# A two-layer graph network on one core: splitting the edge features beforehand and rearranging the attention layer

## The chip, the cores and the metric

The kernel runs on one core of one Trainium2 chip. The core's engines work side by side, each through its own queue of instructions: TensorE (PE), VectorE (DVE), ScalarE (ACT), GpSimd (POOL) and SyncE (SP, which here only issues DMAs). They wait for one another through semaphores. A time is the device time of one execution in microseconds.

## What is computed

A graph of N = 6250 nodes with 16 features, E = 206250 directed edges (each node has a loop edge), 230 edge types. The edges come sorted by dst. Cut to what matters, with h a layer norm and relu of x ahead of each layer:

```python
# layer 0
h_tan = log_map_zero(h)
msg = exp_map_zero(einsum('ei,eio->eo', h_tan[src], rel_weight[etype]) + rel_emb[etype])
lam = 2.0 / (1.0 - c * sum(msg * msg) + EPS)
numer = segment_sum(w * lam * msg, dst);  denom = segment_sum(w * lam, dst)
x = x + mobius_add(project(numer / denom), exp_map_zero(h_tan @ loop_weight))
# layer 1
w_m = (efeat @ W_msg + b_msg).reshape(E, 16, 16);  w_a = (efeat @ W_attn + b_attn).reshape(E, 16, 16)
e1 = w_m * h[src][:, :, None];  e2 = w_a * h[src][:, :, None]
ex = exp(e2 - segment_max(e2, dst)[dst])
attn = ex / segment_sum(ex, dst)[dst]
x = x + segment_sum(e1 * attn, dst).sum(axis=1)
```

## The kernel before

**Tiling.** The nodes are ordered by falling degree into groups of 128, one node to a partition. A window is one group and up to S = 48 consecutive edges of each of its nodes (edge slots, along the free axis). There are 50 windows, run as 25 pairs: the loop body is written out for q = 0 and q = 1, and q chooses the buffer. How many slots a window uses is read from a table (48 in the first, 23 in the last). A block is BLK = 6 slots, a half HALF = 3.

**Prologue** (to about 541 us). TensorE makes a table with one row of 16 floats for each pair of source node and edge type, and SP writes it to DRAM. Index lists srcp (source of each edge) and pairp (row of each edge in that table) are written too, and the raw edge features are copied in DRAM, with 48 rows of padding, into efp (12.9 MB).

**Layer 0** (about 541 to 2935 us). In window k GpSimd waits for the list of indices blkidx, issues 18 gathers (L325, one for each slot, 64 bytes to each partition), then waits for bst_ready and loads blkidx of the window after with pair_block (L320), and issues the rest of the gathers. VectorE, in order: reads the window's word of the table, writes valid (L893), waits for the block load of window k, computes the start and the remainder for window k + 1 (window_start, L873 to L880, which ends in the signal bst_ready), waits for the gathers of window k, and does the math (L903 to L926; ScalarE gives a square root and a tanh in its midst). The signal l0_math at L921 lets GpSimd gather into that buffer again, two windows on. window_start reads two values from the table into registers of VectorE's queue.

**Layer 1** (about 3110 us to the end). Features, weights and biases are split into three bf16 parts each (hi, mid, lo), so that one bf16 product of KE = 100 rows gives fp32 accuracy: hi stands three times, mid twice, lo once, and four more columns carry three ones and the sign of an unused slot (urow makes its score very low). Work of window k:
- GpSimd: the subtraction residue (L376), the loads of source numbers and raw features of the window after (edge_block, L362 and L364), the gathers of rows of h (L325, one for each slot), between them last_part (L380, the low part of the split), at the end the scatter of the finished rows of two windows before (L392).
- ScalarE: the copies of the split (L611, L614), six copies of transposed features from PSUM (L620), the exponential of the carried factor (L633), one exponential for each block of scores (L637, L641).
- TensorE: for each half the attention weights into PSUM (L490), beside them the sums of the exponentials of the window before (exp_sums, L496, products with an identity that add up in the bank psS); then all 48 transposes of the window after (L484), then for each block the message weights and the sums of products (prod_sums, L501).
- VectorE: edge_ids of the window after (L995 to L1000), mold (the maximum carried from the window before, or a very low number where a group begins, L1038), three copies for the finish (L1039 to L1041), window_start two windows ahead, then a score block at a time: two products of weights by h (L1049) and the running maximum (L1061, L1065, L1068). After that the maximum over six slots (L1070), mnew and diff (L1072, L1073), and finish for the window before (L1007 to L1019: total, the sums carried from window to window, is scaled and the sums of psS are added; then ratio and the row of the output). Then the message blocks: scores less maximum (L1089), two products with the message weights (L1049), and their product with the exponentials (L1099), which TensorE adds up.

The order of all engines is written out by hand.

## Time and profile before

| | |
|---|---|
| median of three runs | 6593.14 us (6592.74, 6593.14, 6606.66) |
| the profiled run | 6588.29 us, span 6586.6 us |
| PE busy | 2729.8 us (41%), 13477 instructions |
| PE weight load busy | 1922.8 us (29%) |
| DVE busy | 3678.9 us (56%), 4670 |
| ACT busy | 1293.7 us (20%), 1247 |
| POOL busy | 4382.1 us (67%), 3814 |
| TensorE clock granted | 0.92 on average |
| DMA | 167.76 MB; in layers 0 and 1 some 6 to 12 GB/s |

The span is from the first to the last instruction of the profiled execution; the run took 1.7 us more. Busy is time in which an engine works on an instruction that is not a register, branch, semaphore or DMA-queue one, so time that a queue spends on those is idle time with the reason "issue". The stages have their own limits, so the shares over the whole span say little: they are to be read by stretch.

### The profile page before, as it was taken

How to read it: one execution, taken by the hardware profiler on the slowest of the kernel's cores; microseconds unless marked ns; L12 is line 12 of the kernel's file. 1: busy time of each engine (PE TensorE's matmuls, PEld its weight loads, DVE VectorE, ACT ScalarE, POOL GpSimd, SP SyncE). 2: the span in 40 equal slices, each digit the busy share in tenths (PEclk: the TensorE clock that was granted, in tenths of full speed). 3: DMA queues.
4: the chain of work that ended last, by engine and by line, in shares of the span. 5: the costliest groups of instructions: out<-in, count | busy, mean ns of one | idle time of the engine just before them, and what ended most of it. 6: DMA issues, size and time to landing. Idle time of an engine off the chain costs nothing.

```text
span 6586.6 us, 56916 instructions
## 1 busy us (share of the span) xinstructions
PE 2729.8 (41%) x13477; PEld 1922.8 (29%) x13478; DVE 3678.9 (56%) x4670; ACT 1293.7 (20%) x1247; POOL 4382.1 (67%) x3814
## 2 busy tenths in 40 slices
PE   3530000000000000000567777777777777777676
PEld 1110000000000000000445555555555555555454
DVE  8221111111112111231689989998988898888877
ACT  3530000000000000000222222222222222223222
POOL 0335676767666766656477877777777777776753
PEclk9999999999999999998788888888888888888888
DMA  5880000000000000000000000000000000000000
GB/s 164 275 263 11 6 6 6 6 6 6 6 6 6 6 6 6 6 8 11 6 10 10 12 9 9 9 9 12 9 9 12 9 12 9 12 12 9 12 11 5
DMA packets 141814, 167.76 MB, mean 25 GB/s; under 512 B 73235, under 2 KB 130056, under 8 KB 135287
## 3 DMA queue, kind: packets, MB, share of 16 engines
q0 software_dynamic: 122896, 57.46, 6.2%
q1 hardware_dynamic: 18865, 110.05, 5.2%
q8 instruction: 8, 0.13, 0.0%
q14 instruction: 13, 0.11, 0.0%
q10 hardware_dynamic: 32, 0.01, 0.0%
HBM read 71.76 MB, written 108.57 MB: 27 GB/s over the span
## 4 chain that ended last, share of the span: by engine, by line
POOL 23%; issue 18%; DVE 17%; DVEq 16%; PE 13%; DMA 4%; another core or an unknown queue 4%; POOLq 2%; ACT 1%; SPq 0%; ACTq 0%
POOL gath L325 20%; DVEq L1096 6%; PE psS L501 4%; PE psS L496 4%; DVE stage L1049 4%; PE psW L490 3%; DMA table<-arena 3%; DVEq L1057 3%; DVE arena L1049 2%; DVE work L1070 2%; DVEq L1049 1%; DVE stage L1099 1%; DVE work L673 1%; DVE work L1013 1%
## 5 line engine op out<-in xcount | busy, mean ns | idle before, releaser
L325 POOL DMA_INDIRECT gath<-h_dram,hidx x1695 | 2223.5, 1312 | 509.3 <-issue 509.1
L325 POOL DMA_INDIRECT gath<-table,blkidx x1646 | 1600.0, 972 | 505.7 <-issue 503.0
L484 PE MATMUL psT<-identb,stage 128*100 128x128 bf16 x2448 | 209.5, 255 | 2599.5 <-POOL stage L380 2569.7
L501 PE MATMUL psS<-stage,ident 128*128 128x256 f32 x3390 | 976.3, 447 | 341.8 <-DVE stage L1099 297.7
L484 PEld LDWEIGHTS psT<-identb,stage 128*100 128x100 bf16 x2448 | 190.8, 155 | 2623.9 <-POOL stage L380 2531.5
L501 PEld LDWEIGHTS psS<-stage,ident 128*128 128x128 f32 x3390 | 736.5, 225 | 534.3 <-DVE stage L1099 354.0
L496 PE MATMUL psS<-arena,ident 128*128 128x256 f32 x3390 | 830.4, 382 | 0.0
L490 PE MATMUL psW<-wst,stage 100*128 100x256 bf16 x3390 | 580.0, 292 | 472.2 <-DVE stage L1049 270.0
L673 DVE TENSOR_TENSOR work<-gath 128x768 f32<-128x768 f32 x50 | 47.9, 958 | 1154.1 <-DMA gath<-table,blkidx 1150.8
L496 PEld LDWEIGHTS psS<-arena,ident 128*128 128x128 f32 x3390 | 605.5, 191 | 70.2
L1049 DVE TENSOR_TENSOR arena<-psW,gath 128x768 f32 (+1 forms) x565 | 520.7, 952 | 173.8 <-DMA gath<-h_dram,hidx 58.2
L637 ACT ACTIVATE arena<-arena x271 | 401.9, 1483 | 1019.3 <-DVE arena L1089 989.4
L1099 DVE TENSOR_TENSOR stage<-stage,arena x294 | 498.6, 1696 | 88.7 <-issue 35.3
L620 ACT COPY stage<-psT 100x1024 bf16<-100x1024 bf16 x306 | 289.9, 1026 | 1298.8 <-PE psT L484 1213.6
L1049 DVE TENSOR_TENSOR stage<-psW,gath 128x768 f32 x565 | 513.9, 949 | 24.8 <-remote 24.8
L1089 DVE TENSOR_TENSOR arena<-arena,work 128x1536 f32 (+1 forms) x294 | 496.8, 1690 | 16.2 <-issue 16.2
L490 PEld LDWEIGHTS psW<-wst,stage 100*128 100x128 bf16 x3390 | 287.2, 101 | 725.5 <-DVE stage L1049 325.8
L595 ACT ACTIVATE work<-work 128x48 f32<-128x48 f32 x50 | 12.1, 243 | 2236.7 <-DVE work L905 2092.1
L1065 DVE TENSOR_TENSOR work<-work,arena 128x1536 f32<-128x1536 f32 x171 | 328.6, 1922 | 15.8
L874 DVE SCALAR_TENSOR_TENSOR bstf<-tabs,info 128x1 f32 (+1 forms) x103 | 21.7, 211 | 472.0 <-issue 472.0
L446 PE MATMUL psW<-stage,work 102*125 102x460 bf16 (+1 forms) x400 | 190.9, 617 | 173.1 <-ACT arena L578 141.4
L376 POOL TENSOR_TENSOR efraw<-efraw,stage 128x768 f32<-128x768 f32 x51 | 86.3, 1692 | 236.2 <-DVEq L1000 173.7
(216 smaller groups left out, 2680.3 us busy)
## 6 DMA issues: line engine op xcount, KB each, us to landing
table<-arena SPq DMA_DIRECT2D x50, 1610.0 KB
gath<-h_dram,hidx POOLq DMA_INDIRECT x1695
gath<-table,blkidx POOLq DMA_INDIRECT x1646
efp<-in_edge_attr SPq DMA_DIRECT2D x1, 12890.6 KB
table<-arena SPq DMA_DIRECT2D x50, 186.9 KB
arena<-first_dram POOLq DMA_DIRECT2D x1, 915.5 KB, 12.1
info<-info_dram POOLq DMA_DIRECT2D x2, 432.0 KB, 6.4
arena<-in_dst,rowi POOLq DMA_INDIRECT x51
```

Of the source, the lines that this page charges most:

```text
L325: pool.indirect_dma_start(out=gath[:, q, s, :], out_offset=None, in_=rows, in_offset=bass.IndirectOffsetOnAxis(ap=idx[:, q, s:s + 1].bitca ...
L484: last = nc.tensor.transpose(psTb[0:KE, t % 3, j, 0:GP], efs[:, 8 * t + j, :], identb[0:GP, 0:GP])
L490: last = nc.tensor.matmul(psW[0:GP, h % 2, j * IO:(j + 1) * IO], efT[:, q, h * HALF + j, 0:GP], wst[:, c0:c0 + IO], start=True, stop=True)
L496: nc.tensor.matmul(psS[0:GP, 0:IO], ident[0:GP, 0:GP], score[:, q, s, :], start=False, stop=False)
L501: nc.tensor.matmul(psS[0:GP, IO:2 * IO], ident[0:GP, 0:GP], prod[:, c0:c0 + IO], start=False, stop=False)
L620: nc.scalar.copy(efT[:, q, 8 * t:8 * t + 8, 0:GP], psTb[0:KE, t % 3, :, 0:GP]).then_inc(m["efT_sb"], 1)
L637: nc.scalar.activation(v, v, ACT.Exp).then_inc(m["exp_done"], 1)
L1049: V.tensor_tensor(dst_ap.rearrange("p s (i o) -> p s i o", o=D), psW[0:GP, s, 0:HALF * IO].rearrange("p (s i o) -> p s i o", i=D, o=D), bc ...
L1065: V.tensor_tensor(macc, macc, score[:, q, ds(b * BLK, BLK), :], ALU.max)
L1089: V.tensor_tensor(blk, blk, mnew[:, q, :].unsqueeze(1).to_broadcast([GP, n, IO]), ALU.subtract).then_inc(m["sub_done"], 1)
L1096: V.drain()
L1099: V.tensor_tensor(pr, pr, blk.rearrange("p s c -> p (s c)"), ALU.mult).then_inc(m["q_ready"], 1)
```

## The change

The split of the edge features into bf16 parts no longer happens in each window of layer 1. A new DRAM array ef6 holds, for each edge, its 100 bf16 values (41 MB in all). It is made in 50 chunks during the loop of layer 0: SP loads a chunk of raw features (33 edges to each of 125 partitions), VectorE splits it in four operations behind the math of each window (split_chunk), SP stores it. srcp holds the source number plus one, row 0 of h's array in DRAM is zeros, and unused slots point there. In layer 0 window_start is computed one window earlier.

In layer 1 GpSimd has no arithmetic any more: it loads the source numbers (src_block) and the finished 100-column rows (edge_rows, 9600 bytes to each partition), gathers and scatters. Starts and remainders come from ScalarE (edge_start), and so does mold. The 48 transposes are cut into six parts; two go ahead of the message blocks and one behind the weights of each of the first four blocks, with two PSUM buffers in place of three. ScalarE does the copy of a part behind the exponential of a block. The maximum mnew lies in PSUM. The carried sums are put back into the bank psS by one product of the identity with carry, so the addition to total is gone; the finish follows the first subtraction of the message blocks, and the table's word for the next window is read under its reciprocal. The reduction over six slots has become pairwise maxima, and the three copies at the window's start are gone. The diff, cut to its core and with twelve columns of indentation taken off:

```diff
+        mold, ratio, diff, cfac = (col256(j) for j in range(4))
...
+        carry = efraw[:, 0, 0:2 * IO]
...
+        mnew = psT[0:GP, 8:10, :].rearrange("p a n -> p (a n)")
...
-sp.dma_start(efp_d[0:E * D].rearrange("(a b) -> a b", b=1375),
-             efeat.rearrange("e d -> (e d)").rearrange("(a b) -> a b", b=1375)).then_inc(m["efp_out"], 16)
...
+def chunk_in(rows, j):
+    sp.dma_start(efc[:, j, :, :].rearrange("p r d -> p (r d)"), rows).then_inc(m[f"efc_in{j}"], 16)
+def chunk_out(rows, j):
+    sp.dma_start(rows, ef6[:, j, :, :].rearrange("p r k -> p (r k)")).then_inc(m[f"ef6_out{j}"], 16)
+for j in range(2):
+    chunk_in(efrows[:, j, :], j)
+with sp.Fori(0, ECH // 2 - 1) as t:
+    for j in range(2):
+        sp.wait_ge(m["ef6_split"], t * 2 + (j + 1))
+        chunk_out(ef6rows[:, ds(2 * t + j, 1), :].rearrange("p a n -> p (a n)"), j)
+        chunk_in(efrows[:, ds(2 * t + (j + 2), 1), :].rearrange("p a n -> p (a n)"), j)
...
+def src_block(q):
     pool.indirect_dma_start(out=blkidx[:, q, :], out_offset=None, in_=srcp_d.rearrange("(e a) -> e a", a=1),
...
+                            in_offset=bass.IndirectOffsetOnAxis(ap=ebst[:, q:q + 1].bitcast(U32), axis=0)).then_inc(m[f"src_in{q}"], 16)
+def edge_rows(q):
+    pool.indirect_dma_start(out=efrow, out_offset=None, in_=ef6_d.rearrange("(e k) -> e k", k=KE),
+                            in_offset=bass.IndirectOffsetOnAxis(ap=ebst[:, q:q + 1].bitcast(U32), axis=0)).then_inc(m["ef_in"], 16)
...
-    nc.gpsimd.tensor_tensor(efres, efin, efs[:, :, HI:HI + D], ALU.subtract).then_inc(m["res_done"], 1)
...
-    nc.gpsimd.tensor_tensor(efs[:, :, LO:LO + D], efres, efs[:, :, MID:MID + D], ALU.subtract).then_inc(m["lo_done"], 1)
...
+def next_ids(w, q):
+    pool.wait_ge(m["start_ready"], w + 1)
+    pool.sem_inc(m["passed"], 1)
+    src_block(q)
...
-        residue(k)
-        edge_block(k + 1, 1 - q)
...
-                last_part(k)
+            if b == 1:
+                if q:
+                    next_ids(k + 1, 0)
+                else:
+                    with pool.If(i > 0):
+                        next_ids(k + 1, 1)
...
+        pool.wait_ge(m["efT_ps"], k * (S // 8) + (S // 8))
+        pool.sem_inc(m["passed"], 1)
+        edge_rows(1 - q)
...
+def transposes(w, t):
+    pe.wait_ge(m["efT_sb"], w * (S // 8) + (t + 1))
+    for j in range(8):
+        last = nc.tensor.transpose(psTb[0:KE, t % 2, j, 0:GP], efs[:, 8 * t + j, :], identb[0:GP, 0:GP])
+    last.then_inc(m["efT_ps"], 1)
...
-        transposes(k + 1)
+        pe.wait_ge(m["valid_in"], k + 2)
+        for t in range(2):
+            transposes(k + 1, t)
         pe.wait_ge(m["sum_read"], k + 1)
-        nc.tensor.matmul(psS[0:GP, :], zero[:, 0:GP], zero[:], start=True, stop=False)
+        nc.tensor.matmul(psS[0:GP, :], ident[0:GP, 0:GP], carry, start=True, stop=False)
         for b in range(NBW):
...
+            if b + 2 < S // 8:
+                transposes(k + 1, b + 2)
...
+def edge_start(w, q):
+    g, _ = window(act, w)
+    n = tabs[0:GP, ds(w, 1)]
...
+    A.activation(ebstf[:, q:q + 1], n, ACT.Identity, bias=info[:, ds(g, 1), 2 * D], scale=float(S))
+    A.activation(erem[:, q:q + 1], n, ACT.Identity, bias=info[:, ds(g, 1), 2 * D + 1], scale=-float(S))
...
+    A.activation(ebst[:, q:q + 1], eover[:, q:q + 1], ACT.Identity, bias=ebstf[:, q:q + 1], scale=-1.0)
...
+def copy_T(w, q, t):
+    act.wait_ge(m["efT_ps"], w * (S // 8) + (t + 1))
+    nc.scalar.copy(efT[:, q, 8 * t:8 * t + 8, 0:GP], psTb[0:KE, t % 2, :, 0:GP]).then_inc(m["efT_sb"], 1)
...
 with act.Fori(0, pairs) as i:
     for q in range(2):
         k = 2 * i + q
-        split(k + 1)
-        copies(k + 1, 1 - q)
+        nc.scalar.activation(mold, mnew, ACT.Identity, bias=ekeepbig[:, q:q + 1],
+                             scale=ekeep[:, q:q + 1]).then_inc(m["mold_ready"], 1)
+        nc.scalar.drain()
+        edge_start(k + 2, q)
...
         act.wait_ge(m["d_ready"], k + 1)
...
+        nc.scalar.activation(cfac, diff, ACT.Exp).then_inc(m["c_ready"], 1)
+        for b in range(NBW):
...
+            if b < S // 8:
+                copy_T(k + 1, 1 - q, b)
...
     V.drain()
...
+def split_chunk(t, j):
+    dve.wait_ge(m[f"efc_in{j}"], t * 16 + 16)
+    raw = efc[:, j, :, :]
+    V.tensor_copy(ef6[:, j, :, HI:MID].rearrange("p r (t d) -> p r t d", d=D),
+                  raw.unsqueeze(2).to_broadcast([PN, CHR, 3, D]))
+    V.drain()
+    tt(efres, raw, ef6[:, j, :, HI:HI + D], ALU.subtract)
+    V.tensor_copy(ef6[:, j, :, MID:LO].rearrange("p r (t d) -> p r t d", d=D),
+                  efres.unsqueeze(2).to_broadcast([PN, CHR, 2, D]))
+    V.drain()
+    V.tensor_tensor(ef6[:, j, :, LO:LO + D], efres, ef6[:, j, :, MID:MID + D], ALU.subtract)
+    V.drain().then_inc(m["ef6_split"], 1)
...
-        window_start(k + 1, 1 - q, m["bst_ready"])
+        V.drain()
+        dve.wait_ge(m["blk_in"], 16 * k + 16)
+        dve.sem_inc(m["passed"], 1)
+        window_start(k + 2, q, m["bst_ready"])
...
+        with dve.If(i < ECH // 2):
+            with dve.If(i > 0):
+                dve.wait_ge(m[f"ef6_out{q}"], i * 16)
+                dve.sem_inc(m["passed"], 1)
+            split_chunk(i, q)
...
+def edge_ids(t, q):
+    dve.wait_ge(m[f"src_in{q}"], t * 16 + 16)
+    dve.sem_inc(m["passed"], 1)
+    V.scalar_tensor_tensor(hidx[:, q, :], iotaf[:, 0:S], erem[:, q:q + 1], blkidx[:, q, :], ALU.is_lt, ALU.mult)
+    V.drain().then_inc(m["idx_ready"], 1)
+def edge_valid(w, q):
+    dve.wait_ge(m["ef_in"], 16 * w + 16)
+    dve.sem_inc(m["passed"], 1)
+    V.tensor_scalar(efs[:, :, KE - 1], iotaf[:, 0:S], erem[:, q:q + 1], None, ALU.is_ge)
+    V.drain().then_inc(m["valid_in"], 1)
+def next_code(k):
+    dve.reg_mov(code, dve.value_load(tabgn[:, ds(k, 1)], min_val=0, max_val=GC * GSTEP + GSTEP - 1))
+def finish(q, n, k=None):
+    dve.wait_ge(m["sum_done"], n)
+    V.reciprocal(ratio, psS[0:GP, 0:IO])
+    if k is not None:
+        next_code(k)
+        dve.wait_ge(m["c_ready"], n + 1)
+        V.tensor_tensor(carry.rearrange("p (a c) -> p a c", a=2), psS[0:GP, :].rearrange("p (a c) -> p a c", a=2),
+                        cfac.unsqueeze(1).to_broadcast([GP, 2, IO]), ALU.mult)
     V.drain()
...
-    tt(total, total, cfac[:, q, :].unsqueeze(1).to_broadcast([GP, 2, IO]), ALU.mult)
...
-    V.tensor_tensor(total, total, psS[0:GP, :].rearrange("p (a c) -> p a c", a=2), ALU.add)
+    V.tensor_tensor(ratio, ratio, psS[0:GP, IO:2 * IO], ALU.mult)
     V.drain().then_inc(m["sum_read"], 1)
-    V.reciprocal(ratio, total[:, 0, :])
...
-    tt(ratio, ratio, total[:, 1, :], ALU.mult)
     row_sum(ft[:], ratio.rearrange("p (i o) -> p o i", o=D))
...
+    g = dve.snap(gprev, min_val=0, max_val=GC)
+    V.scalar_tensor_tensor(orow[:, q, :], ft[:], info[:, ds(g, 1), 2 * D + 3],
+                           xnew[:, ds(g, 1), :].rearrange("p a d -> p (a d)"), ALU.mult, ALU.add)
+    V.tensor_copy(oidx[:, q:q + 1], nidx[:, ds(g, 1)])
     V.drain().then_inc(m["fin"], 1)
...
+        v = dve.snap(code, min_val=0, max_val=GC * GSTEP + GSTEP - 1)
+        g, nh = v // GSTEP, dve.snap((v % GSTEP) // 4 + 1, min_val=1, max_val=NHW)
...
-        V.tensor_scalar(mold, mnew[:, 1 - q, :], keep[:, q:q + 1], keepbig[:, q:q + 1], ALU.mult, ALU.add)
-        V.tensor_copy(gx[:, q, 0:D], xnew[:, ds(g, 1), :].rearrange("p a d -> p (a d)"))
-        V.tensor_scalar(gx[:, q, D:D + 1], deg[:, ds(g, 1)], 1.0, None, ALU.min)
-        V.tensor_copy(gid[:, q:q + 1], nidx[:, ds(g, 1)])
...
-        window_start(k + 2, q, m["bst1_ready"])
...
+        edge_valid(k + 1, 1 - q)
+        tt(macc[:, 0:HALF, :], macc[:, 0:HALF, :], macc[:, HALF:BLK, :], ALU.max)
+        dve.wait_ge(m["mold_ready"], k + 1)
+        V.tensor_tensor(macc[:, 0, :], macc[:, 0, :], macc[:, 1, :], ALU.max)
+        V.tensor_tensor(macc[:, 2, :], macc[:, 2, :], mold, ALU.max)
         V.drain()
-        V.tensor_reduce(mred, macc.rearrange("p s c -> p c s"), AX.X, ALU.max)
...
-        tt(mnew[:, q, :], mred, mold, ALU.max)
...
+        tt(mnew, macc[:, 0, :], macc[:, 2, :], ALU.max)
+        V.tensor_tensor(diff, mold, mnew, ALU.subtract).then_inc(m["d_ready"], 1)
+        def from_max(b, n):
+            blk = score[:, q, ds(b * BLK, n), :]
+            V.tensor_tensor(blk, blk, mnew.unsqueeze(1).to_broadcast([GP, n, IO]),
+                            ALU.subtract).then_inc(m["sub_done"], 1)
         def messages(b, halves=2):
             n = halves * HALF
...
             dve.wait_ge(m["q_free"], tb + b + 1)
...
             V.drain()
             dve.wait_ge(m["exp_done"], tb + b + 1)
             pr = prod[:, ds(par, n * IO)]
...
+            V.tensor_tensor(pr, pr, score[:, q, ds(b * BLK, n), :].rearrange("p s c -> p (s c)"),
+                            ALU.mult).then_inc(m["q_ready"], 1)
+        from_max(0, BLK)
+        if q:
+            with dve.If(i > 0):
...
+            finish(0, k, k + 1)
+        else:
...
+            with dve.If(i > 0):
+                finish(1, k, k + 1)
+            with dve.If(i < 1):
+                next_code(1)
+        edge_ids(i + 1, q)
+        messages(0)
+        with dve.Fori(1, nh // 2) as b:
+            from_max(b, BLK)
             messages(b)
```

## Rows read from the trace of the kernel before

**Rows 1.** Busy time by stretch: window and length, engines, clock, DMA share, GB/s.
```profile
0.00:500.00 500.00, 197.36 (x454) 64.24 (x455) 222.36 (x200) 199.62 (x266) 119.92 (x113) 1.00 0.73 231
541.00:2935.00 2394.00, 0.00 (x0) 0.00 (x0) 415.18 (x1190) 150.79 (x197) 1648.24 (x1697) 1.00 0.06 6
3110.00:6580.00 3470.00, 2519.68 (x12958) 1850.90 (x12958) 2991.81 (x3150) 926.77 (x767) 2504.97 (x1895) 0.86 0.06 10
```

**Rows 2.** Groups of GpSimd, 541 to 2935: count | busy, mean | idle before.
```profile
L325 POOL DMA_INDIRECT gath<-table,blkidx x1646 | 1600.0, 972 | 505.7 <-issue 503.0 <-DMA blkidx<-pairp,bst 2.7
L320 POOL DMA_INDIRECT blkidx<-pairp,bst x51 | 48.3, 946 | 268.3 <-remote 178.1 <-DVEq L880 75.3 <-issue 14.9
```

**Rows 3.** Timeline of layer 0, 1500 to 1610: start, duration, operation [idle before].
```profile
1524.04 0.96 DVE L673 TENSOR_TENSOR work<-gath 128x768 f32<-128x768 f32 x1 [24.80 <-DMA gath<-table,blkidx]
1524.22 1.59 POOL L325 DMA_INDIRECT gath<-table,blkidx  x1 [0.30 <-issue]
...
1534.73 0.16 DVE L925 TENSOR_TENSOR lamsum<-lamsum,lsum 128x1 f32 x1
...
1549.42 0.16 DVE L874 SCALAR_TENSOR_TENSOR bstf<-tabs,info 128x1 f32 x1 [11.65 <-issue]
...
1552.29 0.14 DVE L879 TENSOR_SCALAR bst<-bstf 128x1 int32<-128x1 f32 x1
1553.27 0.95 POOL L320 DMA_INDIRECT blkidx<-pairp,bst  x1 [7.13 <-remote]
```

**Rows 4.** Timeline of VectorE in a late window of layer 0.
```profile
2916.24 0.16 DVE L874 SCALAR_TENSOR_TENSOR bstf<-tabs,info 128x1 f32 x1 [0.97 <-issue]
```

**Rows 5.** Timeline of VectorE, 616 to 670: a window without a wait.
```profile
620.64 0.25 DVE L893 TENSOR_SCALAR valid<-iotaf,rem 128x48 f32<-128x48 f32 x1 [1.07 <-issue]
...
636.62 0.96 DVE L673 TENSOR_TENSOR work<-gath 128x768 f32<-128x768 f32 x1 [3.28 <-issue]
...
659.79 0.16 DVE L925 TENSOR_TENSOR lamsum<-lamsum,lsum 128x1 f32 x1 [0.54 <-issue]
667.12 0.25 DVE L893 TENSOR_SCALAR valid<-iotaf,rem 128x48 f32<-128x48 f32 x1 [7.17 <-issue]
668.57 0.16 DVE L874 SCALAR_TENSOR_TENSOR bstf<-tabs,info 128x1 f32 x1 [1.20 <-issue]
```

**Rows 6.** Timeline of VectorE in layer 1, window of 33 slots.
```profile
5137.42 1.82 DVE L1049 TENSOR_TENSOR arena<-psW,gath 128x768 f32<-128x768 f32 x2 [0.31 <-PE psW L490]
...
5158.64 2.80 DVE L1070 TENSOR_REDUCE work<-work 128x256 f32<-128x1536 f32 x1
...
5163.15 0.69 DVE L1011 TENSOR_TENSOR work<-work,psS 128x512 f32<-128x512 f32 x1
...
5195.87 0.96 DVE L1099 TENSOR_TENSOR stage<-stage,arena  x1 [0.22 <-ACT arena L641]
...
5199.61 1.57 DVE L1038 TENSOR_SCALAR work<-work,keep,keepbig 128x256 f32<-128x256 f32 x1 [1.18 <-issue]
...
5203.40 1.82 DVE L1049 TENSOR_TENSOR arena<-psW,gath 128x768 f32<-128x768 f32 x2 [0.31 <-issue]
```

**Rows 7.** Groups of GpSimd in that window.
```profile
L325 POOL DMA_INDIRECT gath<-h_dram,hidx x33 | 44.1, 1337 | 9.9 <-issue 9.9
```

**Rows 8.** Groups of VectorE, 3300 to 6580.
```profile
L1065 DVE TENSOR_TENSOR work<-work,arena 128x1536 f32<-128x1536 f32 x164 | 316.3, 1929 | 15.1
...
L1068 DVE TENSOR_TENSOR work<-work,arena 128x768 f32<-128x768 f32 x23 | 34.9, 1520 | 2.1
```

**Rows 9.** Timeline of layer 1, 6334 to 6400, a late window.
```profile
6358.66 4.50 PE L484 MATMUL psT<-identb,stage 128*100 128x128 bf16 x40 [2.76 <-POOL stage L380]
...
6374.51 1.76 DVE L1099 TENSOR_TENSOR stage<-stage,arena  x1 [6.52 <-issue]
```

**Rows 10.** Timeline of TensorE, 5134 to 5206.
```profile
5135.46 1.46 PE L496 MATMUL psS<-arena,ident 128*128 128x256 f32 x6
...
5188.72 2.86 PE L501 MATMUL psS<-stage,ident 128*128 128x256 f32 x12 [1.35 <-DVE stage L1099]
```

227 lines of the change are left out of this document (99 added, 128 removed).

## The prediction

> **What bounds the kernel now.** I read the busy time by stretch first. It splits the run into a prologue up to 541 us, the message stage of layer 0 (541 to 2935) and the attention stage of layer 1 (3110 to the end) [rows 1]. In layer 0 GpSimd is the only engine that works most of the time, 1648 of 2394 us; in layer 1 VectorE is busy 2992 of 3470 us and GpSimd 2505. So the two stages have different bounds, and the change touches both.
>
> Layer 0, the groups of GpSimd: 1646 gathers of 972 ns, each after about 0.3 us of issue, and 51 block loads of pairp before which GpSimd sat idle for 268 us [rows 2]. Gathers come every 1.25 us, so 33 of them and the block load take 42.5 us, while the mean window is 2394 / 50 = 47.9 us. The timeline says where the rest goes. In a middle window VectorE starts its math at 1524.04 and ends it at 1534.89 (10.9 us), but it writes the last word of the next block's address (L879) at 1552.43, and 0.84 us later GpSimd issues the block load, after 7.13 us without work. Ahead of L874 stand only register loads, a wait long fulfilled and a branch, yet VectorE is idle 11.65 us there, with "issue" as the reason [rows 3]. In a late window the same gap is 0.97 us [rows 4]. So VectorE's queue has two speeds in this stage. In the one window in which VectorE does not wait for gathers at all (its math begins at 636.62) even the math takes 23.3 us for the same instructions as the 10.9 [rows 5]: 12.4 us more over some 15 drains, 0.8 us each, and before L874 10.7 us more over 8 register instructions, 1.3 us each. I can't name the cause from the trace; I take it as a property of the stage: after a long wait VectorE runs about 12 us at full speed and then pays about 1.3 us for each queue instruction until it waits again. This matters more for this forecast than anything in layer 1.
>
> Layer 1, VectorE's timeline: one window of 33 slots runs from its first product at 5137.42 to the next at 5203.40, 66.0 us [rows 6]. The message blocks are a chain of VectorE alone (subtract, two products, product, 5.25 us a block); GpSimd's 33 gathers cost 44.1 us, plus 9.9 us of issue, plus its two subtractions and three other DMAs [rows 7], so it is a close second at about 62 us.
>
> **Layer 1, part by part.** All terms are for each of 50 windows, and on VectorE's path unless said.
> - The window's border. From the end of the last product (5195.87 + 0.96) to the next window's first product 6.57 us pass [rows 6]: three index operations, mold, three copies to gx and gid, window_start with two register loads. The change moves mold and window_start to ScalarE (which is idle there for tens of us), drops the copies, and reads the code word one window ahead under the reciprocal. What stays is a drain, register sums and the loop branch; the nearest row is the issue gap of 1.18 us at the same place. I take 1.35 us (0.8 to 2.4): minus 5.2 us. One index operation comes back inside the window: plus 0.35.
> - The maximum: a reduction of 2.80 us becomes one 128x768 maximum (0.96) and two of 128x256 (some 0.4 each, by 0.69 for the 512 columns of L1011; their ends overlap) [rows 3, 6]: minus 0.95.
> - The sums: a product of 128x512 (0.69) and an addition of 128x512 (0.69) become one product read from PSUM, and the carried sums go back by one TensorE pass: minus 0.7. The bounds here are minus 1.4 (if the product hides under a wait) and plus 1, if TensorE's pass over 512 fp32 columns comes late (three over 256 columns, in six instructions, take 1.46 us, so it takes 1.0) [rows 10].
> - The valid columns: one small write fewer: minus 0.2.
> Sum: minus 6.7 us, times 50 = 335 us.
> - GpSimd's two subtractions vanish. They ran beside VectorE's maxima: over the stage L1065 averages 1929 ns, for 164, where a product of the same 1536 columns takes 1.76 us [rows 9], and L1068 averages 1520 ns, for 23, where 768 columns take 0.96 us [rows 3, 8]: 28 + 13 = 41 us.
> - Windows of 27 and fewer slots, from 6086 on. There the low part of the edge features is ready late, 40 transposes follow at once at 6358.66, and VectorE stands 6.52 us before its first product of messages [rows 9]. With the split done beforehand this goes: about 6 windows by 6.5 = 39 us.
> Together 415 us. New on the path: transposes between the blocks. In a block of 5.25 us TensorE waits 1.35 us for the products [rows 10]; eight transposes take 0.9 (40 in 4.50) [rows 9]. That fits, barely; in stretches at the lower of its two clocks, 1.2 instead of 2.4 GHz, it doesn't (the granted clock is 0.86 on average) [rows 1]. ScalarE gets a copy behind each exponential. I allow 1 us a window for late transposes or exponentials, bounds 0 and 3.6: plus 50 (0 to 180). Layer 1: 415 - 50 = about 370 us less (235 to 415).
> GpSimd: 33 gathers at 1.25 to 1.6 us and three DMAs are 45 to 57 us against VectorE's new 59, so it stays behind; its edge_rows now also waits for six transposes of the block before, about 52 us into the window, and behind it stand only the scatter and the next window's gathers. The rows it loads are 1.2 MB; the prologue moved 231 GB/s on average [rows 1], so some 5 us, needed 25 us later.
>
> **Layer 0, part by part.** Removed: window_start is made one window earlier, so GpSimd's block load no longer waits for VectorE, if VectorE keeps up. The 268 us [rows 2] less the first wait (39) and 0.3 us for each of 50 are 214 us at most. Added: one chunk of the split a window on VectorE, 4 operations of 1584, 528, 1056 and 528 columns. By 0.96 us for 768 [rows 3] they are 2.0 + 0.7 + 1.3 + 0.7 = 4.7 us. Around them stand nine queue instructions: two branches, two waits whose values are computed, four drains and a register sum. At full speed they cost below 1 us, at the slow speed 9 x 1.3 = 12 us, and the operations hide under them. What is queued behind is the next valid, window_start and the math that frees a gather buffer. VectorE's cycle is then 10.9 (math) + 17.6 (up to L879) + 5 (to its wait) + 12 = 46 us, about 48 with the second drain of valid. GpSimd needs n x 1.25 + 2.5 us for n slots; over all windows that is 1646 x 1.25 + 50 x 2.5 = 2183 us. The windows come in falling order, 48 slots first and 23 last; 34 of them have 36 or fewer, 31 on average by the gathers between block loads, and there VectorE's 48 us are 6.6 more than GpSimd's: 226 us. 2183 + 226 = 2409 against 2394: plus 15 us (minus 214 to plus 561, below).
> Prologue: the copy of edge features (12.9 MB) goes, but GpSimd's 50 scatters of 1.5 us set that stretch; a store of src is added ahead of the table. Nothing, within 5 us. The moved split's DMAs, 0.26 MB in and 0.83 MB out a window on SP, meet 16 DMA engines that are busy 6% [rows 1]; nothing.
>
> **The sum.** The profiled run took 6588.3 us (span 6586.6), 5 us under the median 6593.1. 6593 - 370 + 15 = 6238, so 6240.
>
> **The rivals.**
> 1. VectorE's queue runs at full speed in layer 0 (because SP now works beside it, or because it is less often behind). Then layer 0 is GpSimd's alone: 6593 - 370 - 214 = 6010. For it: late windows do run fast [rows 4]. Against it: some 45 of 50 show the slow speed.
> 2. Slower than before: VectorE falls behind, never waits, and never gets its full speed back. The window without a wait took from 620.64 to 667.12, 46.5 us [rows 5]; with 12 us more it is 58.5, and 50 of them 2925 to 2955 against 2394: plus 561 at most. 6593 - 370 + 561 = 6785. It decides against the change from 55.3 us a window in layer 0 on (370 / 50 above 47.9). Against it: as soon as GpSimd had issued nothing for some us (around 661 to 667) VectorE went fast again (the gap before L874 was 1.20 us), and a VectorE that is the bound makes GpSimd silent.
> 3. Layer 1 gives half: transposes at the lower TensorE clock and edge rows that land late put 3.7 us more into each window. 6593 - 185 + 15 = 6423.
> 4. The split slows the gathers. The mean gather of layer 0 is 972 ns and stands 0.3 us behind the last [rows 2]; those that start beside one of VectorE's wide SBUF operations are the long ones, as the one of 1.59 us beside the product of 1524.04 [rows 3], up to 0.65 more than the others. Four more such operations a window hold GpSimd up 2.6 us, 130 us in all if it is the bound: 6370. The Trainium skill, SBUF — State Buffer, section Who interferes with whom, says more: a copy or cast on VectorE that uses both ports blocks GpSimd's descriptor writes for its whole length, while a product of two SBUF tensors takes only the read side. No row here has a large cast beside a gather; by that rule the two casts would cost up to 3.3 us a window, 6405.
> That the change doesn't do what it says could only be so for the gathers: GpSimd's count of them stays 1695 and 1646.
>
> **Chances.** Forecast 0.42 (6120 to 6350), rival 1 0.20, rival 2 0.14, rival 3 0.14, rival 4 0.10. The range 6000 to 6620 leaves out rival 2 and a little more. Under 0.2% (13 us) no change can be told; that case needs layer 0 to eat layer 1 almost exactly, 0.02. Faster 0.84, slower 0.14.
>
> **What would show it.** Right: from the end of one window's last product to the next first product below 2 us in layer 1; VectorE's windows of 33 slots at 58 to 60 us; no POOL operation but DMAs; no 6.5 us gap from 6100 us on; in layer 0 no idle GpSimd before the pairp load, and its idle time moved to the start of a window, before the gathers, in windows of under 33 slots. Wrong: VectorE's math in layer 0 at 23 us in most windows (rival 2), or windows there of n x 1.25 + 2.5 us throughout (rival 1); TensorE or ScalarE named as the releaser of VectorE's message products (rival 3).

## The result and the profile after

The changed kernel took 8111.6 us (median of four runs, 8076 to 8126) against 6592.9: 1.232 times the time, 95% interval 1.229 to 1.236 (the two medians alone give 1.230). The forecast was 6240, range 6000 to 6620.

The runs were measured in seven sessions. The runs of one kernel in one session lie within 2%, but sessions differ: the kernel before took 6593 us here and 6550, 6579 and 6546 in three of the sessions below, and 6280, 6280 and 6276 in three others. I call them slow-queue sessions and free sessions, for VectorE's slow queue of layer 0 [rows 3, 5] is in every trace of the first kind and in none of the second (layer 0 takes 2384 to 2412 us in the 13 traces of the first, 2175 to 2229 in the 7 of the second). This result and the profile of before are from the first kind.

First the page of the changed kernel: its head, the slices of VectorE and GpSimd, and three groups.

```profile
span 8074.7 us, 56866 instructions
...
PE 2997.2 (37%) x13527; PEld 2055.4 (25%) x13528; DVE 3566.0 (44%) x4214; ACT 1210.8 (15%) x1559; POOL 3655.3 (45%) x3713
...
DVE  7312221222222333446545655555555555555565
...
POOL 1157666776767654443333334333333333333331
...
L1120 DVE TENSOR_TENSOR arena<-psW,gath 128x768 f32 (+1 forms) x565 | 531.5, 954 | 2192.8 <-remote 1591.9
...
L387 POOL DMA_INDIRECT stage<-ef,ebst x51 | 48.0, 941 | 2241.8 <-PE psT L509 2241.1
...
L655 ACT COPY stage<-psT 100x1024 bf16<-100x1024 bf16 x306 | 301.3, 997 | 88.5 <-remote 73.4
```

Then its busy time by stretch (as [rows 1]):

```profile
541.00:2935.00 2394.00, 0.00 (x0) 0.00 (x0) 565.69 (x1283) 150.80 (x197) 1662.18 (x1693) 1.00 0.12 28
3110.00:8070.00 4960.00, 2785.38 (x13008) 1982.46 (x13008) 2725.11 (x2611) 844.04 (x1060) 1771.07 (x1803) 0.75 0.07 16
```

VectorE's work in layer 1 is less, 2725 us for 2992, yet the stage takes 5017 us from the first gather of h to the end, where before took 3538: plus 1479. Layer 0, from its first gather to the last addition to lamsum, takes 2406 for 2397. The whole loss is idle time of VectorE before its score products: 2193 us at L1120, where the kernel before has 174 at its L1049. Of the 2193, 1592 are "remote": a semaphore ended the wait, but no instruction in the profile had ended just before. GpSimd's 2241 us at L387 are a long wait too, but behind it stand gathers whose buffer isn't free yet.

The timeline of VectorE in a window of 33 slots, and under it TensorE's:

```profile
5658.59 1.76 DVE L1162 TENSOR_TENSOR stage<-stage,arena  x1
5663.94 0.96 DVE L1120 TENSOR_TENSOR arena<-psW,gath 128x768 f32<-128x768 f32 x1 [3.60 <-issue]
5665.57 0.96 DVE L1120 TENSOR_TENSOR arena<-psW,gath 128x768 f32<-128x768 f32 x1 [0.67 <-PE psW L515]
5669.80 0.96 DVE L1120 TENSOR_TENSOR arena<-psW,gath 128x768 f32<-128x768 f32 x1 [3.27 <-PE psW L515]
5679.69 0.96 DVE L1120 TENSOR_TENSOR arena<-psW,gath 128x768 f32<-128x768 f32 x1 [8.93 <-remote]
5680.74 1.76 DVE L1131 TENSOR_TENSOR work<-arena 128x1536 f32<-128x1536 f32 x1
5692.67 0.96 DVE L1120 TENSOR_TENSOR arena<-psW,gath 128x768 f32 x1 [10.17 <-remote]
```

```profile
5660.40 2.86 PE L526 MATMUL psS<-stage,ident 128*128 128x256 f32 x12 [2.18 <-DVE stage L1162]
...
5668.29 0.49 PE L515 MATMUL psW<-wst,stage 100*128 100x256 bf16 x3
...
5670.81 0.50 PE L515 MATMUL psW<-wst,stage 100*128 100x256 bf16 x3 [0.73 <-DVE arena L1120]
...
5680.70 0.82 PE L515 MATMUL psW<-wst,stage 100*128 100x256 bf16 x3 [8.09 <-DVE arena L1120]
```

The fourth product starts at 5679.69; the weights that it waits for stand at 5668.29 to 5668.78 in TensorE's row, 10.9 us earlier, and VectorE has been free since 5670.76. The fifth starts at 5692.67, 21.4 us after its own weights (5670.81 + 0.50), which stood in the other buffer; VectorE idled 10.17 us of that. TensorE in turn stands until a product frees a buffer.

What is late is TensorE's signal. The trace also records when a semaphore rises: w_ready, for which these two products wait, rises at 5679.66 and at 5692.41, so VectorE starts 0.03 and 0.26 us after its signal, but the signal comes 10.9 and 21.1 us after the matmuls. The weights that end at 5681.52 are signalled at 5708.54, 27 us later; those that end at 5710.64 are signalled at 5710.65. ScalarE's copies of TensorE's transposes (L655 above) wait for such signals too, 73 us in all.

GpSimd's gathers run through all of it. Here are the first and the last of the burst, and VectorE's products around its end:

```profile
5661.19 0.97 POOL L350 DMA_INDIRECT gath<-h_dram,hidx  x1 [8.71 <-DVEq L1185]
...
5703.59 0.94 POOL L350 DMA_INDIRECT gath<-h_dram,hidx  x1 [0.30 <-issue]
```

```profile
5708.80 0.96 DVE L1120 TENSOR_TENSOR arena<-psW,gath 128x768 f32 x1 [15.17 <-remote]
5709.85 1.76 DVE L1134 TENSOR_TENSOR work<-work,arena 128x1536 f32<-128x1536 f32 x1
5711.52 1.82 DVE L1120 TENSOR_TENSOR arena<-psW,gath 128x768 f32 x2
```

The last gather began at 5703.59; five microseconds later the products follow one another again. A window goes from its first score product to the next window's. I count it as slow when VectorE idles more than 30 us in it: 45 of windows 3 to 49, against none before.

The first two windows are left out of this count, for there the kernel before has the same thing. Its VectorE and its TensorE at the start of layer 1, with gathers every 1.25 us beside them:

```profile
3117.85 0.96 DVE L1049 TENSOR_TENSOR arena<-psW,gath 128x768 f32 x1 [0.62 <-issue]
3122.59 0.96 DVE L1049 TENSOR_TENSOR arena<-psW,gath 128x768 f32 x1 [3.79 <-remote]
...
3130.99 0.96 DVE L1049 TENSOR_TENSOR arena<-psW,gath 128x768 f32 x1 [5.59 <-remote]
3139.44 0.96 DVE L1049 TENSOR_TENSOR arena<-psW,gath 128x768 f32 x1 [7.50 <-remote]
```

```profile
3114.24 1.69 PE L490 MATMUL psW<-wst,stage 100*128 100x256 bf16 x6 [0.30 <-issue]
3118.86 0.82 PE L490 MATMUL psW<-wst,stage 100*128 100x256 bf16 x3 [2.94 <-DVE arena L1049]
3123.61 0.82 PE L490 MATMUL psW<-wst,stage 100*128 100x256 bf16 x3 [3.92 <-issue]
```

The last three products start 6.7, 11.3 and 15.0 us after their weights ended (3115.93, 3119.68, 3124.43). In the second window one waits 15.4 us. A product is called late below when it waits more than 1.5 us and the reason is "remote": the kernel before has 10, the changed kernel 159, and the seven traces of free sessions none.

### The profile page after: what moved, and what is told of

The parts are those of the page before. It is cut to its first block, busy times and chain, and to the rows that moved or that the text cites. A ratio compares the mean times of both kernels' runs of the same rounds, so it can differ in the third digit from the quotient of the medians.

```text
span 8074.7 us, 56866 instructions
## 1 busy us (share of the span) xinstructions
PE 2997.2 (37%) x13527; PEld 2055.4 (25%) x13528; DVE 3566.0 (44%) x4214; ACT 1210.8 (15%) x1559; POOL 3655.3 (45%) x3713
## 4 chain that ended last, share of the span: by engine, by line
issue 22%; another core or an unknown queue 21%; DVEq 20%; DVE 15%; PE 13%; POOL 4%; DMA 4%; ACT 1%; SPq 0%; POOLq 0%; ACTq 0%
PE psS L526 6%; DVEq L1159 5%; PE psS L521 4%; POOL gath L350 3%; DVE stage L1120 3%; DMA table<-arena 3%; DVE arena L1120 2%; PE psW L515 2%; DVE stage L1162 2%; DVEq L1127 2%; DVEq L1087 1%; DVE work L722 1%; DVEq L723 1%; DVEq L1120 1%
## 5 line engine op out<-in xcount | busy, mean ns | idle before, releaser
L350 POOL DMA_INDIRECT gath<-h_dram,hidx x1695 | 1664.6, 982 | 866.7 <-issue 516.8
L1120 DVE TENSOR_TENSOR arena<-psW,gath 128x768 f32 (+1 forms) x565 | 531.5, 954 | 2192.8 <-remote 1591.9
L515 PE MATMUL psW<-wst,stage 100*128 100x256 bf16 x3390 | 628.4, 311 | 1696.5 <-DVE arena L1120 869.9
L387 POOL DMA_INDIRECT stage<-ef,ebst x51 | 48.0, 941 | 2241.8 <-PE psT L509 2241.1
L521 PE MATMUL psS<-arena,ident 128*128 128x256 f32 x3390 | 1027.6, 449 | 27.4 <-issue 27.2
L526 PE MATMUL psS<-stage,ident 128*128 128x256 f32 x3390 | 934.3, 432 | 162.6 <-DVE stage L1162 161.6
L526 PEld LDWEIGHTS psS<-stage,ident 128*128 128x128 f32 x3390 | 708.3, 216 | 316.2 <-DVE stage L1162 204.5
L521 PEld LDWEIGHTS psS<-arena,ident 128*128 128x128 f32 x3390 | 735.3, 232 | 149.9 <-issue 32.8
L658 ACT ACTIVATE arena<-arena 128x1536 f32<-128x1536 f32 (+1 forms) x294 | 421.4, 1433 | 980.7 <-DVE arena L1149 979.4
L1120 DVE TENSOR_TENSOR stage<-psW,gath 128x768 f32 (+1 forms) x565 | 514.3, 950 | 16.7 <-issue 14.8
L1162 DVE TENSOR_TENSOR stage<-stage,arena (+1 forms) x294 | 498.6, 1696 | 30.4 <-ACT arena L658 4.6
L1149 DVE TENSOR_TENSOR arena<-arena,psT 128x1536 f32 (+2 forms) x294 | 495.3, 1685 | 0.0
L655 ACT COPY stage<-psT 100x1024 bf16<-100x1024 bf16 x306 | 301.3, 997 | 88.5 <-remote 73.4
L1134 DVE TENSOR_TENSOR work<-work,arena 128x1536 f32<-128x1536 f32 x171 | 300.7, 1758 | 15.8
L558 PE MATMUL psS<-efraw,ident 128*128 128x512 f32 x100 | 102.7, 1130 | 286.5 <-DVEq L1089 281.2
```

The costliest lines, as they stand in the source:

```text
L350: pool.indirect_dma_start(out=gath[:, q, s, :], out_offset=None, in_=rows, in_offset=bass.IndirectOffsetOnAxis(ap=idx[:, q, s:s + 1].bitca ...
L515: last = nc.tensor.matmul(psW[0:GP, h % 2, j * IO:(j + 1) * IO], efT[:, q, h * HALF + j, 0:GP], wst[:, c0:c0 + IO], start=True, stop=True)
L521: nc.tensor.matmul(psS[0:GP, 0:IO], ident[0:GP, 0:GP], score[:, q, s, :], start=False, stop=False)
L526: nc.tensor.matmul(psS[0:GP, IO:2 * IO], ident[0:GP, 0:GP], prod[:, c0:c0 + IO], start=False, stop=False)
L655: nc.scalar.copy(efT[:, q, 8 * t:8 * t + 8, 0:GP], psTb[0:KE, t % 2, :, 0:GP]).then_inc(m["efT_sb"], 1)
L658: nc.scalar.activation(v, v, ACT.Exp).then_inc(m["exp_done"], 1)
```

## The experiments

Theory A, after this trace: at the window's border VectorE now stands still for 3.6 us (TensorE finishes its last sums first); GpSimd's burst of gathers starts right then; VectorE, waiting for TensorE, falls into a stall that feeds itself and lasts as long as gathers go back to back. Rivals: B, gathers without GpSimd's own arithmetic between them do it in any phase; C, some other part of the new score phase is slow.

**a_late1, a_late2: the burst later.** GpSimd waits for a signal of VectorE; in a_late1 at the first maximum (shown), in a_late2 behind diff, at the end of the score phase.

```diff
+pool.wait_ge(m["go"], k + 1)
...
 V.tensor_tensor(macc, score[:, q, 0:BLK, :], score[:, q, BLK:2 * BLK, :], ALU.max)
+    .then_inc(m["go"], 1)
```

> The changed kernel; in layer 1 GpSimd may start the gathers of a window only when VectorE has done the first maximum of the window it works on, some 9 us after the window's start, instead of right at its start. Theory A (the burst of gathers meets a VectorE that stands still for 3.6 us at the window's border and waits for TensorE; that starts a slow state which feeds itself): VectorE is in full swing when the burst begins, windows of 33 slots fall from 97 us to 62 to 66, and the whole time to 6300 to 6600. Theory B (gathers issued back to back make TensorE's signals late for VectorE in whatever phase they meet it): the slow stretch only moves 9 us on, windows stay above 85 us, the whole above 7500. Theory C (something else in the score phase is slow, such as ScalarE's silence or the maximum in PSUM): no change, 8050 to 8150.

> The changed kernel; the gathers start only when VectorE has done the maximum of the window (its score phase is over), so the score phase of 20 us runs without gathers and the message phase of 35 us with them. Gathers of 33 slots need 42 to 50 us, so they reach beyond the end of the window and VectorE waits for them: 20 + 45 = 65 to 70 us a window in both A and the case where message blocks bear the burst; the whole 6500 to 6900. Theory B: the message phase becomes slow too, above 90 us a window, above 7500 in all. Theory C: the score phase stays slow although no gather runs in it, 8000 and more.

a_late1: 6497 us, 0.9915 of before (0.988 to 0.995), no slow window. a_late2: 7555, 30 slow windows, now in the message phase (887 us of "remote" ahead of its products). So it isn't the score phase as such (C falls), nor any burst (B falls with a_late1, though a_late2 came as B said, above 7500, and not at A's 6500 to 6900); neither is it only the border, since a late burst finds another place.

**a_busy, a_busy1: no stand of VectorE at the border.** Two (one) maxima of 1536 columns, unused, ahead of the wait for the gathers.

```diff
+for _ in range(2):
+    tt(macc, score[:, q, 0:BLK, :], score[:, q, BLK:2 * BLK, :], ALU.max)
 dve.wait_ge(hgath[q], dve.snap(cum[q]) * (16 * HALF))
```

> The changed kernel; VectorE does two maxima of 1536 columns (1.76 us each, result unused) ahead of its wait for the gathers at each window's start, so it stands still 3.6 us less there; the gathers start at the same time as before. Theory A: the slow state is not entered in most windows, whole time 6300 to 6900. Theory B or a form of A in which any wait for TensorE in the burst will do: still above 7700, 3.5 us a window more at most.

> The changed kernel with one maximum of 1536 columns (1.76 us, result unused) ahead of VectorE's wait for the gathers, where a_busy had two. Theory A (VectorE standing still when the burst begins starts the slow state): the stand is halved to 1.8 us; if that is short enough the time is a_busy's less 50 times 1.75, 6365; if it isn't, some or all windows fall back to 90 us and more, 6700 to 8100. Theory A' (what counts is only that the first wide operation on VectorE comes soon after the first gather): 6365 too.

a_busy: 6453 beside 6550, one slow window: with 3.5 us of useless work in each window the kernel is 97 us faster than before, where the changed kernel was 1519 slower. a_busy1: 6815 beside 6579, 7 slow windows, others half way. Where the fill covers the stand, TensorE gets two halves of weights ahead as well, so the two can't be told apart here.

**b_nosub: the kernel before, GpSimd without its subtractions** (the middle and low parts of the features are zero), and window_start of layer 0 one window earlier.

```diff
-nc.gpsimd.tensor_tensor(efres, efin, efs[:, :, HI:HI + D], ALU.subtract).then_inc(m["res_done"], 1)
+pool.sem_inc(m["res_done"], 1)
...
-window_start(k + 1, 1 - q, m["bst_ready"])
+window_start(k + 2, q, m["bst_ready"])
```

> The kernel before with two edits. In layer 1 GpSimd's two subtractions are left out (the middle and low parts of the features are zero), so GpSimd only gathers, and VectorE's order and its full border stay. Theory A: VectorE has no gap of more than 1.2 us at the border, so windows of 33 slots stay at 60 to 66 us. Theory B: they go to 85 us and more, as in the changed kernel. In layer 0 window_start is made one window earlier, without the split of the edge features: my prediction's terms give GpSimd's own pace or VectorE's cycle of 10.9 + 17.6 + 5 + 2 = 36 us, whichever is longer, so layer 0 takes 2180 to 2230 us instead of 2394; if VectorE's slow queue still rules it, 2350 to 2420.

6555 beside 6550, no slow window: B falls again. Layer 0 took 2384 us, not 2180 to 2230: most of its first 30 windows took 50 to 55 us whatever their slots, while the long ones of the changed kernel took 63 to 67. The split costs VectorE some 12 us a window there, as priced.

**a_wait1, a_pace: the first product, and the rate.** GpSimd begins behind VectorE's first product; or waits for the landing of each three gathers.

```diff
 # a_wait1
+if first and s == 0:
+    dve.sem_inc(m["go"], 1)
...
 # a_pace
 gather(h2_d, hidx, q, b, HALF, hgath)
+pool.wait_ge(hgath[q], pool.snap(ch[q]) * 48 + (48 * b + 48))
```

> The changed kernel; GpSimd may start a window's gathers only when VectorE has gone past its first product of the window in progress, so VectorE has had its stand of 3.6 us before the burst begins, and nothing is added on any engine. Theory A: the time is that of a_busy without its 175 us of added work, 6280 to 6330, below the kernel before (some 6550 on that chip). Theory B' (any wait of VectorE for TensorE inside the burst starts the slow state; the first products of a window wait about 1 us each for TensorE): 7500 to 8100.

> The changed kernel; GpSimd waits after each three gathers of layer 1 until they have landed, so they are no longer back to back: about 1.5 to 2 us more for each three, 33 gathers in 58 to 63 us. The start of the burst and VectorE's stand stay. Theory A with the rate as its cause (only gathers back to back starve VectorE and TensorE): windows of 33 slots 62 to 68 us, the whole 6400 to 6750. If the start alone decides and the rate does not, the slow state stays and lasts as long as the longer burst: windows of 110 us and more, 8500 and above.

a_wait1: 6904, 1.053 of before (1.046 to 1.060). Three windows are slow, but in most of the others VectorE idles 8 to 13 us in the score phase, where the changed kernel without late signals has 3.7 and the kernel before 2.5. A as I had it (only the stand, 6280 to 6330) falls, and so does the forecast of 7500 to 8100 for any wait; a burst that begins 0.9 us after the first product does harm as long as VectorE waits for TensorE at each product. a_pace: 6938, above the 6400 to 6750 expected, for VectorE now waits 938 us for gathers, which the pauses make too slow; but none of its products is late. So the rate of the gathers matters.

**b_gap: a stand of VectorE in the kernel before.**

```diff
 window_start(k + 2, q, m["bst1_ready"])
+with dve.If(i < 24):
+    dve.wait_ge(m["src_in"], 16 * k + 48)
```

> The kernel before with one wait added on VectorE: ahead of the first product of a window of layer 1 it waits for the landing of the block of source numbers that GpSimd loads just then at the head of its gathers, so VectorE stands still for 2 to 3 us as the burst begins, as in the changed kernel; all else (GpSimd's subtractions, the maximum, the transposes) is as before. Theory A: the slow state appears here too, many windows at 90 us and more, the whole above 7300. Rival (it takes another part of the change, such as ScalarE's silence in the score phase or the maximum in PSUM): windows grow by 2 to 3 us only, 6650 to 6750.

6778 beside 6579: the stand is there (3.6 us, as in the changed kernel) and costs about its own time, no slow window, 8 late products. TensorE had its two halves of weights ready. The theory that is left, A'': the stalls start when a burst runs while VectorE waits for TensorE product by product.

**a_pace2, b_tight, b_tight_ns, a_busy_r.** The pause only behind the first two threes; and in the kernel before a TensorE that isn't ahead, with and without GpSimd's subtractions (without them the middle and low parts are zero).

```diff
 # a_pace2
+if b < 2:
+    pool.wait_ge(hgath[q], pool.snap(ch[q]) * 48 + (48 * b + 48))
...
 # b_tight, b_tight_ns
 pe.wait_ge(m["efT_sb"], k * (S // 8) + (S // 8 + 3))
+pe.wait_ge(m["bst1_ready"], k + 3)
```

> The changed kernel; GpSimd waits for the landing of its gathers after the first and after the second three of each window of layer 1, the rest goes back to back. Theory A'' (the slow state starts when a burst of gathers without pauses meets the first four products of a window, where VectorE waits for TensorE's weights product by product, and later products, for which TensorE is ahead, don't start it): no slow window, GpSimd's window grows by some 4 us to 55 and stays behind VectorE's 60; total 6280 to 6350, 3 to 4% below the kernel before. If a burst can start the slow state at any wait: a part of the windows at 90 us and more, 6500 to 7500.

> The kernel before with one wait added on TensorE: it begins with a window's weights only when VectorE has ended window_start, just ahead of its first product, so TensorE is no longer ahead at the window's start and VectorE waits for it at each of the first four products, as in the changed kernel, while the gathers begin. GpSimd keeps its two subtractions and starts its first gather 3 us after VectorE's first product. Theory A'': slow windows appear, at least in part, above 6900. If GpSimd's own arithmetic and its late start are cover enough: 2 to 5 us more a window, 6680 to 6830.

> The same wait on TensorE, in the kernel of b_nosub (GpSimd's two subtractions left out, so the middle and low parts of the features are zero, and window_start of layer 0 one window earlier). Now nothing of the change is in layer 1 but GpSimd that only gathers and a TensorE that is not ahead. Theory A'': slow windows of 85 us and more, the whole above 7000. If another part of the change is needed (the maximum or the sums in PSUM, ScalarE, the spread transposes): 6650 to 6800.

6133 (0.9765 of before, 0.975 to 0.978), 6409 and 6296; a_busy again: 6134 (0.9766). But the kernel before, measured beside them, took 6280, and layer 0 of b_tight, whose code is that of before, 2180 us for 2397. It was a free session, so none of these tested the slow windows. Hence the changed kernel itself went into the next sessions.

> The changed kernel unchanged, beside the kernels of this call. The kernel before took 6550 to 6590 us in two calls and 6280 in the third, with windows of layer 0 at GpSimd's own pace in the third: VectorE's slow queue was absent there. If the slow queue of layer 0 and the slow windows of layer 1 are one property, and it depends on where or when the kernel runs, then: where the kernel before takes 6550 and more, the changed kernel takes 8000 to 8150; where it takes about 6280, the changed kernel has no slow windows and takes 5980 to 6080 (2225 us of layer 0 and some 3120 of layer 1). If they are two properties, 7700 to 7850 beside a kernel before of 6280.

> The kernel of a_pace2 again. Beside a kernel before of 6280 it took 6133. Beside one of 6550 and more: 6300 to 6400 if the pause of GpSimd's first six gathers keeps the slow windows away, 6500 to 7500 if it doesn't.

> The kernel of b_tight_ns again (it leaves GpSimd's two subtractions out). Beside a kernel before of 6280 it took 6296. Beside one of 6550 and more, theory A'' expects slow windows of 85 us and more and a time above 7000; without them 6570 to 6650.

In that session before took 6546. The changed kernel: 7821, 1.197 (1.193 to 1.201), 36 slow windows. a_pace2: 6387, 0.9758 (0.974 to 0.977), none. This pair is the strongest evidence here: two pauses of some 2 us a window, in the same session, take away 1434 us. b_tight_ns: 6688, three slow windows, where A'' wanted most windows slow and more than 7000: that forecast missed. In one of the three VectorE's timeline has the late products of the changed kernel:

```profile
4342.44 1.76 DVE L1066 TENSOR_TENSOR work<-work,arena 128x1536 f32<-128x1536 f32 x1
4346.35 0.96 DVE L1050 TENSOR_TENSOR arena<-psW,gath 128x768 f32 x1 [2.14 <-remote]
4351.30 0.96 DVE L1050 TENSOR_TENSOR arena<-psW,gath 128x768 f32 x1 [4.00 <-remote]
4352.35 1.76 DVE L1066 TENSOR_TENSOR work<-work,arena 128x1536 f32<-128x1536 f32 x1
4356.98 0.96 DVE L1050 TENSOR_TENSOR arena<-psW,gath 128x768 f32 x1 [2.88 <-remote]
```

**after_r2, b_early.** The changed kernel once more, and b_tight_ns with six gathers ahead of the block loads (the middle and low parts zero again).

```diff
-residue(k)
-edge_block(k + 1, 1 - q)
 for b in range(MINH):
     gather(h2_d, hidx, q, b, HALF, hgath)
+    if b == 1:
+        residue(k)
+        edge_block(k + 1, 1 - q)
```

> The kernel of b_tight_ns (the kernel before; TensorE not ahead at the window's start; GpSimd's two subtractions left out), and GpSimd issues the first six gathers of a window ahead of its two block loads, so the burst begins some 5 us before VectorE's first product instead of 2.7 us behind it, as in the changed kernel. Nothing of the maximum, the sums, the transposes or ScalarE's new work is in it. If the trigger is a burst under way while VectorE waits for TensorE product by product: beside a kernel before of 6550 most windows are slow (85 us and more), 7300 to 8100. If the two full slow windows of b_tight_ns were chance and another part of the change counts: 6600 to 6750.

> The changed kernel again. Beside a kernel before of 6550 and more: 7700 to 8150, as in the two calls so far. Beside one of about 6280 (no slow queue in layer 0): 5980 to 6080 if the slow windows of layer 1 come with the same condition, 7400 to 7850 if not.

A free session again, before 6280. The changed kernel: 6118 us, 0.9742 (0.971 to 0.977), no slow window; 5980 to 6080 was expected. b_early 6295, and in a last session, free too (before 6276), 6303: it says nothing of the stalls. VectorE's timeline of the changed kernel in the free session, a window of 33 slots:

```profile
4903.07 0.96 DVE L1162 TENSOR_TENSOR stage<-stage,arena  x1 [0.19 <-ACT arena L658]
4908.10 0.96 DVE L1120 TENSOR_TENSOR arena<-psW,gath 128x768 f32<-128x768 f32 x1 [4.07 <-PE psW L515]
4909.73 0.96 DVE L1120 TENSOR_TENSOR arena<-psW,gath 128x768 f32<-128x768 f32 x1 [0.67 <-PE psW L515]
4911.35 0.96 DVE L1120 TENSOR_TENSOR arena<-psW,gath 128x768 f32<-128x768 f32 x1 [0.67 <-PE psW L515]
4912.98 0.96 DVE L1120 TENSOR_TENSOR arena<-psW,gath 128x768 f32<-128x768 f32 x1 [0.67 <-PE psW L515]
4914.03 1.76 DVE L1131 TENSOR_TENSOR work<-arena 128x1536 f32<-128x1536 f32 x1
4915.70 1.82 DVE L1120 TENSOR_TENSOR arena<-psW,gath 128x768 f32 x2
```

and its busy time by stretch:

```profile
541.00:2765.00 2224.00, 0.00 (x0) 0.00 (x0) 570.70 (x1294) 152.56 (x200) 1690.82 (x1696) 1.00 0.15 31
2920.00:6110.00 3190.00, 2517.34 (x13008) 1859.44 (x13008) 2710.58 (x2611) 844.08 (x1060) 2206.68 (x1805) 0.86 0.12 24
```

The same 2611 operations of VectorE in layer 1 take 2711 us busy here and 2725 there; the stand at the border, the waits of 0.67 us and the gathers under them are the same. Only the 10 us waits are missing, and ScalarE's copies wait 16.9 us in all, none of it "remote".

| windows 3 to 49 | mean window | slow | late products, all windows | burst begins, from the first product |
|---|---|---|---|---|
| before | 68.6 us | 0 | 10 | 3 us after, TensorE ahead |
| changed kernel | 99.7 | 45 | 159 | 1.6 to 4.5 us ahead |
| a_wait1 | 73.4 | 3, others half slow | 66 | 0.9 after |
| b_tight_ns_r | 70.5 | 3 | 15 | 2.7 after |
| a_late1 | 66.2 | 0 | 20 | behind the fourth product |
| a_busy | 65.7 | 1 | 23 | ahead, TensorE ahead too |
| a_pace2_r | 64.2 | 0 | 12 | ahead, with two pauses |
| changed kernel, free session | 63.2 | 0 | 0 | 1.7 to 4.4 us ahead |

All but the last are from slow-queue sessions.

## Why the prediction was wrong

- **The step that failed** is in the sum of layer 1, minus 370 us: it lets VectorE run beside GpSimd's gathers at no cost, and it leaves the slowness of layer 0 there ("I take it as a property of the stage"). The runs showed plus 1479 us in its place (5017 for 3538): beside gathers that follow one another without a pause TensorE's signals came late (by 27 us in the window shown), and VectorE idled 2193 us before its score products for 174. With two pauses in the gathers the same kernel took 6387 for 7821, and in the free sessions it was 6118. No rival had this.
- **The sign was in the trace of the kernel before.** [rows 6] is a window without late signals; the first two windows of layer 1 have them (3122.59 to 3139.44 above).
- **One thing or two.** Every one of the 13 traces with the slow queue in layer 0 has late signals of TensorE in layer 1 (a_pace one, at ScalarE), and none of the 7 others has. That the two are one mechanism is not shown: a slow queue instruction costs about 1.3 us, a late signal 10 to 27 in the window shown.
- **Why 45 windows here and none before** is argued and not shown. The change took away two things: TensorE was ahead of VectorE at a window's start, and the burst began 3 us behind the first product. Each alone does little: the early burst in b_gap (0.2 us ahead of the first product, no slow window) and a_busy (4 us ahead, one), TensorE not ahead in b_tight_ns_r (three).
- **The border.** I left 1.35 us of queue work on the path. The traces show 3.60 and 4.07 in the windows above and 2.4 to 6.2 in all, 3.7 in the middle: VectorE waits for TensorE, which does the last block's sums (2.86 us at L526, a row of [rows 10] that I read for another purpose) before the next window's weights. Then three products wait 0.67 us each. That is some 2.4 us at the border and, against the 2.5 us that the kernel before idles in its score phase, 1.2 us behind it: 3.6 us a window or 180 us more than my sum. My sign of being right, below 2 us, failed too.
- **Layer 1 without the stalls.** In free sessions the stage takes 3242 us; before has no profile there, but 6280 less 545, 2180 and 105 us leaves about 3450. Minus 208, where I had minus 370 (235 to 415). In slow-queue sessions a_pace2_r takes 3323 for 3538, minus 215. Windows of 33 slots: 60 to 63 for 65 to 66, forecast 58 to 60. The border's 180 us cover the missing 160; what gives 20 back isn't separated. GpSimd's subtractions gone, the 1536-column maxima take 1.76 us (L1134, 1758 ns on the page) where they averaged 1929, as priced.
- **Layer 0.** Plus 9 us against a forecast of plus 15, but by another picture, so the near hit is luck. I saw 48 us as VectorE's cycle in every window. In the trace 15 windows take 62 to 67 us and 23 take 19 to 47, mean 48: for some windows VectorE doesn't wait for gathers (rival 2, whose window of 58.5 is 63 to 67), then it runs fast when GpSimd has fallen silent, as its counter-argument said. The math takes 23 us or more in 25 of the 50 windows, and in one in the kernel before. A window in which it takes 24.7 (1351.75 to 1376.42):

```profile
1344.81 0.16 DVE L929 SCALAR_TENSOR_TENSOR bstf<-tabs,info 128x1 f32 x1 [10.30 <-issue]
...
1351.75 0.96 DVE L722 TENSOR_TENSOR work<-gath 128x768 f32<-128x768 f32 x1 [4.04 <-issue]
...
1376.26 0.16 DVE L992 TENSOR_TENSOR lamsum<-lamsum,lsum 128x1 f32 x1 [1.23 <-issue]
1383.95 1.01 DVE L942 CAST arena<-arena 125x1584 bf16<-125x1584 f32 x1 [7.53 <-issue]
```

- **Rival 1** (full queue speed in layer 0, 6010) is what the free sessions are; there before is 6280 too, and the change gives 6118. In them the split costs 43 us of layer 0 (2223 for the 2180 of b_tight).
- **Rival 4** (the split slows the gathers, 130 us). In the slow-queue session the gathers of layer 0 average 982 ns for 972: 16 us in all. In the free sessions they average 999 for the 973 of b_tight, 43 us in all, which is the whole cost of the split there: the rival's mechanism, at a third of its price. The cast of 1584 columns took 1.01 us, half my 2.0. The Trainium skill (SBUF — State Buffer, Who interferes with whom), whose rule stood beside this rival, says that where VectorE's two-port mode and GpSimd want the shared ports, the one that comes second is blocked for the whole instruction. Gather by gather the trace agrees: the one that began at 1384.34, beside the cast that ended at 1384.96, took 1.39 us, and the 98 beside a cast in the free session 1.28 on average, where others take 0.94. But a cast meets only a part of a gather, so the two casts cost less than their 1.01 and 0.73 us.
- **Rival 3** (TensorE or ScalarE late in the message phase) didn't happen: ahead of its message products (L1120 into stage) VectorE idles 17 us in all.

**What stays open.** What holds TensorE's signals back: the record of w_ready shows that they are late, not where. Whether the coupling alone makes slow windows common in the kernel before: b_early, which has both the early burst and a TensorE that isn't ahead, would have told, but its two sessions were free ones. Whether another part of the change (the maximum in PSUM, the spread transposes) counts: no run takes one out. And what makes a session a slow-queue one: two chips, by their numbers, gave one of each kind, 33 and 18 minutes apart.

## What to carry to other kernels

A border between iterations that looks like waste may be what lets the producer engine get ahead; before it is emptied, look up what the next engine (here TensorE with its last sums) still has to do, and which burst starts at that moment. When a trace shows an unexplained slow mode, look for its signs in the other stages' first windows as well, and give it a chance of its own in the forecast of every stage that has its ingredients. Measure the kernel before again beside every experiment: here that alone told the free sessions from the others. The cheap cure here was to let GpSimd pause at the start of its burst (a_pace2): 2.4% faster than the kernel before in both kinds of session, where the changed kernel is 2.6% faster in one and 20 to 23% slower in the other.
